# A graph kernel with fewer, longer scattered rows: groups of 1024 edges, a new order of the loop, a head rebuilt around one-hots laid out by column

## The reference

```
# layer 0 (a second self-loop is added to every node)
deg = count(src) + 1 ;  d = deg ** -0.5
x1  = layernorm(x + segment_sum(x[src] * d[src] * d[dst], dst) + self-loop term)
# layer 1, per edge e = (src, dst)
gate = silu(edge_attr_40 @ W1.T + b1) @ W2.T + b2
gate = gate + sum(emb[type[src]] * (emb[type[dst]] @ adaptW.T))
cw   = where(w < 6, 0.5 * (cos(pi * w / 6) + 1), 0)
msg  = gate * x1[dst] * cw * node_vec[dst]
agg  = segment_sum(msg, src) / segment_sum(node_vec[dst], src)
out  = layernorm(x1 + layernorm(x1 + agg) * gamma + beta)
```

## Time and profile before

| | us |
|---|---|
| median of 3 runs | 3585.37 (3585.33 to 3587.16) |
| the profiled execution, its time | 3596.59 |
| its span | 3594.8 |
| first gather starts / last gather starts / last scatter starts | 410.62 / 3092.20 / 3214.90 |
| the last reduction's first comparison | 3239.27 |
| span after the reduction | 92 |
| granted TensorE clock, mean | 0.832 |

### The profile page before, as it was taken

The page is one execution under the profiler, slowest core; times in us unless marked ns, Lnnn a source line. Parts: engine busy times, 40 slices in busy tenths (PEclk is TensorE's granted clock), DMA queues, the critical chain, the costliest instruction groups (busy, mean ns, idle before and its releaser), DMA issues. The chain is left out here.

```text
span 3594.8 us, 69567 instructions
## 1 busy us (share of the span) xinstructions
PE 2457.2 (68%) x24398; PEld 2030.9 (56%) x24398; DVE 2434.8 (68%) x5609; ACT 1044.9 (29%) x2117; POOL 2265.9 (63%) x2116
## 2 busy tenths in 40 slices
PE   4899256677676767767677766767776767746760
PEld 3677145556555655656555655655555655646660
DVE  7755457777676776777776776777676777746654
ACT  0000123333333333333333333333333333421110
POOL 8700477777777777777777777777777777410002
PEclk9999987888788888888887877887887888868885
DMA  8000323333333333333333333333333333318871
GB/s 312 9 0 0 80 68 97 99 99 97 99 101 97 100 101 93 95 106 95 94 106 93 97 104 94 97 100 98 96 104 94 97 104 95 87 46 325 304 271 13
DMA packets 135012, 383.77 MB, mean 107 GB/s; under 512 B 53904, under 2 KB 53904, under 8 KB 128016
## 3 DMA queue, kind: packets, MB, share of 16 engines
q0 software_dynamic: 79200, 179.69, 18.7%
q1 hardware_dynamic: 53188, 198.17, 16.2%
q10 hardware_dynamic: 2284, 1.33, 0.1%
HBM read 258.83 MB, written 120.22 MB: 105 GB/s over the span
## 5 line engine op out<-in xcount | busy, mean ns | idle before, releaser
L630 POOL DMA_INDIRECT slot<-table,gidx x1616 | 1651.0, 1022 | 517.4 <-issue 485.0
L734 PEld LDWEIGHTS route<-parts,oh_r 128*128 128x128 bf16 x9696 | 810.1, 113 | 73.2 <-ACT routed L779 28.8
L734 PE MATMUL route<-parts,oh_r 128*128 128x148 bf16 x9696 | 828.8, 255 | 33.1 <-ACT routed L779 26.3
L779 ACT ACTIVATE routed<-route 128x444 bf16<-128x444 f32 x808 | 433.4, 541 | 770.4 <-PE route L734 763.7
L639 POOL DMA_INDIRECT perm<-routed,sidx x404 | 436.7, 1081 | 225.2 <-issue 207.1
L899 DVE TENSOR_SCALAR oh_r<-iota_r,spot 128x768 bf16<-128x768 f16 x1616 | 546.7, 413 | 5.2
L701 PE MATMUL rank<-oh_b,before 128*128 128x408 bf16 x202 | 87.7, 434 | 494.6 <-DVE oh_b L860 494.6
L870 DVE TENSOR_REDUCE spot<-rank 128x8 f32<-128x408 f32 x202 | 116.9, 579 | 407.9 <-PE rank L707 407.9
L701 PEld LDWEIGHTS rank<-oh_b,before 128*128 128x128 bf16 x202 | 20.2, 100 | 609.5 <-DVE oh_b L860 607.4
L668 PE MATMUL gate<-w,hid 97*128 97x96 f32 x1616 | 238.4, 294 | 161.2 <-DVE val L984 161.2
L828 ACT ACTIVATE parts<-val 128x392 bf16<-128x392 f32 x202 | 109.5, 542 | 746.3 <-DVE val L994 746.3
(11 more groups left out here) (209 smaller groups left out, 3502.7 us busy)
## 6 DMA issues: line engine op xcount, KB each, us to landing
rows<-perm SPq DMA_DIRECT2D x51, 1554.0 KB, 8.0
oh_t<-dst_row SPq DMA_DIRECT2D x101, 512.0 KB
attr<-in_edge_attr SPq DMA_DIRECT2D x101, 320.0 KB
slot<-table,gidx POOLq DMA_INDIRECT x1616
perm<-zeros SPq DMA_DIRECT2D x51, 444.0 KB, 13.6
perm<-routed,sidx POOLq DMA_INDIRECT x404
table<-tab SPq DMA_DIRECT2D x3, 676.0 KB, 4.7
xin<-in_x SPq DMA_DIRECT2D x1, 1224.0 KB, 9.8
```

The lines of the kernel that those rows point to most:

```text
L630: e.indirect_dma_start(out=slot[:, s, g, :], out_offset=None, in_=table0, in_offset=bass.IndirectOffsetOnAxis(ap=gidx[:, s, g:g + 1], axis ...
L734: mm = e.matmul(route[:, bank, RC * j:RC * (j + 1)], oh_r[:, GR * g + q, bank * R // 2 + j, :], parts[:, s % 2, GR * g + q, :], start=(q = ...
L779: e.activation(routed[:, s % 2, g, bank * ROW // 2:(bank + 1) * ROW // 2], route[:, bank, 0:ROW // 2], ACT.Copy).then_inc(rows_ok, 1)
```

## The change

Sizes: `GR` 4 to 8 (two groups of 1024 edges in a tile), `R` 6 to 10, `CAP` 896 to 1024. Two chunks of nodes share one bucket: `NB` = 26 buckets, and the key of an edge has 8 bits. A scattered row has 10 x 148 values (2960 bytes). `routes` has 160 matmuls a tile in four phases for each group (3, 3, 2, 2 places), and `put_routed` as many copies.

Head: the counting one-hots have three buffers; ACT copies `oh_hi` into `by_col`, with the bucket innermost, and PE's moving operand is read from there; there are 8 group matmuls of 104 columns in place of 4 of 204. `dst` is rounded on ACT; the inverse root is three Newton steps on DVE; constants and the fault test come after the counting loop. The padded `src` and `dst` numbers and the node queries are stored to DRAM. The edge-weight curve, `base`, `fixed`, `w16`, `dst_row` and the keys are computed at the start of the second block, in memory of `oh_r` and `routed`, while POOL's gathers already run.

Main loop: SP loads the indices and the edge weights of each tile from DRAM. The node multiplier is picked as three parts directly into `parts`. `ranks` is one step for a whole tile, at lag 3, and `before16` is folded into `lowered`. All lags and orders change, and the routing of the two groups is separate on PE, ACT and DVE.

Last reduction: 26 loads of 1024 rows; each is used for two halves of 128 nodes, with the keys shifted by 128 for the second, 80 columns a half.

The core of the diff:

```diff
-GR = 4
+GR = 8
-R = 6
+R = 10
-CAP = 896
+CAP = 1024
+NB = (NP2 + 1) // 2
+PHASES = ((0, 3), (3, 6), (6, 8), (8, 10))
+NPH = len(PHASES)
+OR = 3
...
# head, ACT and PE
+def lay(i, s):
+    t = U * i + s
+    e.wait_ge(oh_ready, 2 * (t + 1))
+    if since(i, s, OR):
+        e.wait_ge(oh_used, t - OR + 2)
+    e.activation(by_col[:, s % OR], oh_hi[:, s % OR].rearrange("p b g -> p g b"), ACT.Copy
+                 ).then_inc(laid, 1)
 def count(i, s):
     t = U * i + s
-    e.wait_ge(oh_ready, 2 * (t + 1))
+    e.wait_ge(laid, t + 1)
     for g in range(G):
-        e.matmul(deg[:, 0:NP2], oh_lo[:, s % 2, :, g], oh_hi[:, s % 2, :, g],
+        e.matmul(deg[:, 0:NP2], oh_lo[:, s % OR, :, g], by_col[:, s % OR, g, 0:NP2],
                  start=False, stop=False, skip_group_check=True)
-    by_group = oh_hi[:, s % 2, :, :].rearrange("p b (g q) -> p g q b", q=GR)
+    by_group = by_col[:, s % OR].rearrange("p (g q) b -> p g q b", q=GR)
     for q in range(GR):
         mm = e.matmul(tot[0:NT], band[:, bass.ds(NT - 1 - t, NT)], by_group[:, :, q, :],
...
# head, DVE
+for _ in range(3):
+    done(e.tensor_tensor(near_1[:, :], dinv[:, :], dinv[:, :], ALU.mult))
+    done(e.tensor_tensor(near_1[:, :], near_1[:, :], half[:, :], ALU.mult))
+    done(e.scalar_tensor_tensor(dinv[:, :], near_1[:, :], 1.5, dinv[:, :], ALU.add, ALU.mult))
...
# loop, SP
+def index(i, s):
+    if since(i, s, U):
+        e.wait_ge(gathered[s], 16 * G * i)
+    e.dma_start(gidx[:, s, :], src_pid[:, bass.ds((U * i + s) * G, G)]).then_inc(index_in[s], 16)
+def weigh(i, s):
+    ...
+    e.dma_start(weight[:, s, :], weights[:, bass.ds(t * G, G)]).then_inc(weight_in[s], 16)
-over_tiles(e, NT, U, (load, 0), (rows, 0))
+over_tiles(e, NT, U, (index, 0), (load, 4), (rows, 4), (weigh, 4))
# loop, POOL
-wait_apart(e, gx, t + 1, passed)
+wait_apart(e, index_in[s], 16 * (i + 1), passed)
-over_tiles(e, NT, U, (gather, 0), (scatter, 5))
+over_tiles(e, NT, U, (gather, 0), (scatter, 6))
# loop, PE
+def ranks(i, s):
+    ...
+    e.matmul(at, lowered[:, :], mine, start=True, stop=False, skip_group_check=True)
+    for k in range(1, GR):
+        e.matmul(at[:, :, :, k:GR], ones16[:, :], mine[:, :, :, 0:GR - k], start=False,
+                 stop=False, skip_group_check=True)
+    e.matmul(at, ident_r[0:NT, bass.ds(t, 1)].broadcast_to([NT, P]), ...)
-def routes(g0, g1):
+def routes(g):
     def step(i, s):
         t = U * i + s
-        if g0 == 0:
-            e.wait_ge(split_ok, 3 * (t + 1))
+        e.wait_ge(split_ok, 3 * t + g + 2)
+        e.wait_ge(ohr, NG * t + g + 1)
+        for phase, (a, b) in enumerate(PHASES):
+            n = NPH * (NG * t + g) + phase
+            if since(i, s, 1) or g or phase >= 2:
+                e.wait_ge(rows_ok, n - 1)
+            for j in range(a, b):
+                for q in range(GR):
+                    mm = e.matmul(route[:, phase % 2, RC * (j - a):RC * (j - a + 1)],
+                                  oh_r[:, GR * g + q, j, :], parts[:, s % 2, GR * g + q, :],
+                                  start=(q == 0), stop=(q == GR - 1))
+            mm.then_inc(routing, 1)
-over_tiles(e, NT, U, (layer1(0), 3), (ranks(0), 3), (routes(0, 2), 4), (layer1(1), 3),
-           (rows_of_groups, 3), (ranks(1), 3), (routes(2, NG), 4), (pick(0), 3),
-           (layer2(0), 3), (pick(1), 3), (layer2(1), 3), (total, 0))
+over_tiles(e, NT, U, (layer1(0), 4), (pick(0), 4), (layer2(0), 4), (pick(1), 4),
+           (layer1(1), 4), (routes(0), 5), (layer2(1), 4), (rows_of_groups, 4),
+           (routes(1), 5), (ranks, 3), (total, 0))
# loop, ACT
-over_tiles(e, NT, U, (take_sums, 1), (silu(0), 3), (put_routed(0, 2), 4), (silu(1), 3),
-           (window, 1), (put_routed(2, NG), 4), (put_got(0), 3), (put_high(0), 3),
-           (put_got(1), 3), (put_high(1), 3), (put_middle(0), 3), (put_middle(1), 3))
+over_tiles(e, NT, U, (take_sums, 1), (silu(0), 4), (put_got(0), 4), (put_got(1), 4), (silu(1), 4),
+           (put_routed(0, 0, NPH), 5), (window_high, 1), (put_high(0), 4),
+           (put_routed(1, 0, 2), 5), (window_middle, 1), (put_middle(0), 4),
+           (put_high(1), 4), (put_routed(1, 2, NPH), 5), (window_halves, 1), (put_middle(1), 4))
# loop, DVE (messages is cut into keys, product, less_high, less_middle)
-over_tiles(e, NT, U, (indices, 0), (buckets, 6), (onehots, 3), (steps_of_groups, 6),
-           (normalize, 4), (spots(0), 6), (less_first, 4), (spots(1), 6), (less_second, 4),
-           (put_rows, 6), (route_onehots, 6), (messages, 6))
+over_tiles(e, NT, U, (spots, 5), (keys, 5), (product(0), 5), (normalize, 2), (steps_of_groups, 5),
+           (onehots, 0), (buckets, 4), (route_onehots(0), 5), (put_rows, 5), (less_first, 2),
+           (less_high(0), 5), (product(1), 5), (less_second, 2), (places, 4),
+           (less_high(1), 5), (less_middle(0), 5), (route_onehots(1), 5), (less_middle(1), 5))
...
# last reduction, ACT and DVE
-for b in range(NP2):
+for h in range(NP2):
+    b, s, landed = bucket_of(h)      # h // 2, h // 2 % RS, 16 * (h // 2 // RS + 1)
-    e.activation(mine[:, b % 2], rows[:, b % RS, :, RC - 1], ACT.Copy).then_inc(keyed, 1)
+    e.activation(mine[:, h % 2], rows[:, s, :, RC - 1], ACT.Identity,
+                 bias=shift[:, h % 2:h % 2 + 1]).then_inc(keyed, 1)
-    e.tensor_tensor(onehot[:, b % 2], count42[:, :, :], bc_mid(mine[:, b % 2], P), ALU.is_equal)
+    e.tensor_tensor(onehot[:, h % 2], count[:, :, :], bc_mid(mine[:, h % 2], P), ALU.is_equal)
```

More of the change, by code:

```diff
@@ L447, in _ @@
-                    node_f, chunk, less = (room[:, K * k:K * (k + 1)] for k in range(3))
-                    done(e.tensor_copy(node_f, src_i[:, :]))
-                    done(e.tensor_scalar(pid_i[:, :], node_f, SHIFT + 0.5, 1.0 / H, ALU.add, ALU.mult))
-                    done(e.tensor_copy(chunk, pid_i[:, :]))
-                    done(e.scalar_tensor_tensor(less, chunk, -float(H), node_f, ALU.mult, ALU.add))
-                    done(e.tensor_scalar(less, less, -float(SHIFT), None, ALU.is_lt))
@@ L453, in _ @@
-                    done(e.tensor_tensor(chunk, chunk, less, ALU.subtract))
-                    done(e.scalar_tensor_tensor(node_f, chunk, 2.0, node_f, ALU.mult, ALU.add))
-                    done(e.tensor_scalar(pid_i[:, :], node_f, float(SHIFT), None, ALU.add))
-                    low_i = less.bitcast(I32)
+                    e.wait_ge(src_in, 16)
+                    e.tensor_copy(src_f[:, :], src_i[:, :])
+                    done(e.tensor_scalar(twice[:, :], src_i[:, :], SHIFT + 0.5 - H / 2, 1.0 / H, ALU.add, ALU.mult))
@@ new lines, in _ @@
+                    done(e.tensor_scalar(bad16[:, :], bad[:, :], 0.0, None, ALU.is_gt))
+                    e.nop().then_inc(bad_ok, 1)
+                    e.wait_ge(counted, 1)
+                    done(e.tensor_scalar(deg1[:, :], deg[:, 0:NP2], 1.0, None, ALU.add))
+                    e.tensor_scalar(half[:, :], deg1[:, :], -0.5, None, ALU.mult)
+                    done(e.tensor_scalar(near_1[:, :].bitcast(I32), deg1[:, :].bitcast(I32), 1, None,
+                                         ALU.logical_shift_right))
@@ L594, in build @@
+            nv_r = ssum[:, 0, 0:NP2]
+            d2 = ssum[:, 1, 0:NP2]
+            turned = route[:, :, :].bitcast(BF16)
             HC = G // 2
@@ L825, in step @@
                             e.wait_ge(val_ok, n + 1)
[L826 to L828 removed]
+                            e.activation(parts[:, s % 2, m * HC:(m + 1) * HC, 0:C], val[:, m], ACT.Copy
                                          ).then_inc(high, 1)
@@ new lines, in _ @@
+                    done(e.tensor_tensor(d2, dinv[:, :], dinv[:, :], ALU.mult))
+                    done(e.tensor_scalar(d2, d2, 1.0, None, ALU.add))
+                    e.wait_ge(all_at, 64)
+                    done(e.tensor_tensor(base[:, :, :], x_s, bc_last(d2, C), ALU.mult))
+                    e.wait_ge(a_own, ROUNDED)
+                    e.scalar_tensor_tensor(turn, dist, 1.0 / (2 * CUTOFF), turn, ALU.mult, ALU.subtract
+                                           ).then_inc(rest_ok, 1)
```

750 lines of the change are left out of this document (409 added, 341 removed).

## The result

The changed kernel takes 3540.0 us (3536.8 to 3545.9, 4 runs) beside a kernel before of 3586.3 (3585.3 to 3589.7): ratio 0.987, 95% interval [0.985, 0.989]. It is faster by 46 us, 1.3%, where 348 were forecast and the range ended at 3420. The profiled execution has a span of 3544.1 us, 50.7 less than before.

| stretch | before | forecast | after | change |
|---|---|---|---|---|
| start to first gather | 410.6 | 231 | 248.3 | -162 |
| first gather to end of the last | 2682.5 | 2475 | 2736.7 | **+54** |
| to end of the last scatter | 122.7 | 108 | 101.2 | -22 |
| to the end | 378.9 | 426 | 458.0 | +79 |

A forecast was written before the change was run, and what follows sets the result against it. POOL, issuing without a pause, was taken to bound the main loop. The terms -180 - 200 - 15 + 47 = -348 us gave 3249 us for the profiled execution, 3237 for the median, range 3165 to 3420.

The forecast's parts named there:

- term 2: Main loop: two of four scatters a tile go, POOL stays the bound at 24.7 us a tile; -200 us.
- the leak: Main loop: 0.3 us a tile added for what leaks from DVE's uneven tiles despite POOL's lead.
- E: Main loop: the ring of waits across engines does not open, 30.5 us a tile, 3823 us; 6%.
- C: Main loop: PE and DVE become the bound at 26 to 27 us a tile, 3419 us; 15%.
- Rival D: Main loop: longer one-hots lock POOL out, 0.4 us for each operation beside them, 27.0 us a tile, 3469 us; 6%.
- the rule: Main loop: by the Trainium skill, a fast VectorE tensor_scalar blocks GpSimd for its whole instruction; sum as in Rival D.
- Term 4: Last reduction: DVE takes the transfers' place as bound, 5.9 us a half; +47 us.
- Term 1: Up to the first gather: counting at 1.75 us a tile, first gather at 231 us; -180 us.
- B: Counting stage: stays slow at 3.1 us a tile because PE's matmul cost is not the stride, 3373 us; 8%.
- Term 3: Drain, last gather to last scatter: 108 us where it was 123; -15 us.

The follow-up runs named there:

- kernel with the steps apart: Changed kernel with oh_d moved ahead of the first product, oh_b behind the normalization, step_at between oh_b and route one-hots: 3373.0 us beside 3592.3, ratio 0.940.
- the old kernel's row: Kernel before with oh_d moved from ahead of step_at to directly ahead of its sixteen route one-hots: 3661.5 us beside 3591.6, ratio 1.020.

## Why the prediction was wrong

The step that failed is in term 2: "They cover 7.5 us for 5.4, for which I add 0.3 us a tile: 24.4." It took the cost of a POOL operation beside DVE from single pairs, 1.01 us beside the one-hots and 1.49 behind the large one, and added them up. The pairs were read rightly, but the change also moved the large one-hot ahead of the route one-hots, with oh_b alone between, and a row is not the sum of its pairs. Measured, in us a tile above the floor: 2.85 for what begins in oh_d, where it was 0.31 and I left it; 1.10 in the route one-hots, where it was 0.29 and I added 0.6 with the leak. That is 2.54 + 0.21 us, less a little in the others, for the 2.6 us by which the loop's mean (2736.7/101 = 27.1) missed 24.5. The kernel with the steps apart shows the first part: 0.56 in place of 2.85, 25.2 us a tile. Shown, then: POOL is held over rows of DVE instructions, and this order costs some 170 us beside the one with the three steps apart. The holds of 5.7 us and more that come in nearly every second tile were seen only with oh_d, alone or with oh_b, directly ahead of the row; shorter ones (2.47, 2.7 and 4.22 us) begin inside a row of one-hots, in the kernel with the steps apart with no oh_d near. Not shown: what decides whether a row holds. The normalization ahead and a route wait fulfilled early go together with the holds behind oh_d, the moment at which POOL's operation begins with those inside the old kernel's row, and no run varies one of them alone.

The rest of the loop was right. POOL stayed the bound with 0.30 us of "issue"; a scatter with rows of 2960 bytes takes 1054 ns, one with rows of 1776 bytes 1077; the one-hots take 0.47 us each, as forecast; the ring opened (E) and PE and DVE only follow POOL (C). Rival D had the engine pair and nearly the size, 27.0 us and 3469, but by its mechanism, each operation waiting most of one one-hot, the kernel with the steps apart would have stayed there. The Trainium skill, "SBUF — State Buffer", section "Who interferes with whom", says that a VectorE instruction in a two-port mode, which a tensor_scalar can have, keeps the shared pair for its whole instruction. A tensor_tensor such as oh_d has no such mode by that page, which infers that it leaves the writing of descriptors alone. The traces differ from both: an operation that begins in oh_d goes on at oh_d's end at the earliest (1.90 us, 0.82 of them behind it), and it can be held over nine and more instructions further (5.7 to 6.8 us). The measurement decides. I had set the rule aside because one row, 0.06 us, spoke against it.

Term 4, +79 for +47: "PE's 42 matmuls take 2.94 us, 80 take 5.5" carried the duration over to another layout. At a pitch of 160 bytes a matmul takes 0.081 us, so PE sets 6.48 us a half where DVE at 5.9 was to: 51 x 0.58 = 30 us of the 32 by which the term missed. The order of the bounds (transfers no longer) was right.

Term 1, -162 for -180: the contiguous operand did what was said (16 matmuls in 1.18 us, 8 in 0.57, so B fell), but a tile takes 1.88 us for 1.75. ACT's copy, forecast at 0.9, takes 1.8 and is the longest part of it; DVE, which was to set the pace, waits for PE ahead of many of its one-hots. Counting ended at 216 us for 197: 13 us by the pace, and 7 in the first four tiles, beside POOL's passes at 18 to 29 us. The first gather came 7.8 us after the issue of its index load, where I had put 2 us for that load, with no row behind it. Term 3, -22 for -15: right.

## What to carry to other kernels

Where GpSimd issues without a pause, read not the mean of its operations but their longest, and ask what VectorE wrote in a row at that time; then try the large two-byte comparisons in another order. Here three steps moved together brought 167 us; what a float32 operation between them does alone was not measured, and a fulfilled wait inside the old kernel's row did not let GpSimd in. When steps are reordered, list the new neighbours on each engine as one lists the new waits. And take a matmul's duration only from a row with the same layout of weights.
